# Set-up of a fused attention and soft-MoE kernel: order of the small VectorE steps, and what the first latent products wait for

## The reference, cut to what matters

```python
x = L0_attn_x                                   # (8, 512, 256) float32
x = _layernorm(x + _L0_attn_ref(x, ...), axis=-1)
x = _layernorm(x + _L0_ffn_ref(x, ...), axis=-1)

def _L0_attn_ref(x, ...):                       # 16 heads of 16, latent width 32
    qkv = x @ c_attn_w.T + c_attn_b
    q, k, v = jnp.split(qkv, 3, axis=2)
    q_lat = q @ q2l_w.T + q2l_b                 # k_lat, v_lat likewise with kv2l
    q_lat = q_lat * cos + _rotate_half(q_lat) * sin
    k_lat = k_lat * cos + _rotate_half(k_lat) * sin
    q_for_k = q_lat @ wqk_w.T + wqk_b
    att = softmax(causal(q_for_k @ k_lat^T * L ** (-0.5)))
    y = (att @ v_lat) @ l2o_w.T + l2o_b
    return y @ cproj_w.T + cproj_b

def _L0_ffn_ref(x, ...):                        # 16 experts of 64 slots
    x = _layernorm(x, norm_g, norm_b)
    se = _layernorm(slot_embeds, slot_g, slot_b) * scale
    logits = jnp.einsum('bnd,esd->bnes', x, se)
    ...                                         # dispatch, gated experts, combine
```

## Time and profile before

| | |
|---|---|
| median of 3 runs | 1321.32 us (1320.03 to 1323.57) |
| the profiled execution's own time | 1322.98 us |
| its span, first to last instruction | 1321.3 us |
| PE busy | 1221.5 us, 92% of the span |
| DVE, ACT, POOL busy | 814.6, 681.2, 449.7 us (62%, 52%, 34%) |
| mean granted TensorE clock | 0.957 of full speed |

### The profile page before, as it was taken

One profiled execution on the slowest core, in us unless ns is written; L12 is line 12 of the kernel. 1 busy time (PEld: TensorE's weight loads), 2 busy tenths in 40 slices (PEclk: granted clock), 3 DMA queues, 4 the chain that ended last, 5 costly groups with the idle time before them and its releaser, 6 DMA issues.

```text
span 1321.3 us, 19946 instructions
## 1 busy us (share of the span) xinstructions
PE 1221.5 (92%) x7222; PEld 945.8 (72%) x7222; DVE 814.6 (62%) x1318; ACT 681.2 (52%) x1042; POOL 449.7 (34%) x336
## 2 busy tenths in 40 slices
PE   5799999999999999987799999995999999989996
PEld 4465666666666666654688888884888888879885
DVE  3876697879787978651767777762544444432343
ACT  2445465656565655636477777762555555530111
POOL 5454555465646555402000000000544444430000
PEclk8898999999999999987799999997999999999998
DMA  4644363545445453601043333225655555453771
GB/s 122 138 98 108 89 160 88 150 105 142 117 115 143 113 141 88 160 15 64 33 160 112 112 112 112 96 96 190 201 165 166 162 166 164 136 195 97 226 250 48
DMA packets 121791, 170.32 MB, mean 129 GB/s; under 512 B 47025, under 2 KB 76146, under 8 KB 121714
## 3 DMA queue, kind: packets, MB, share of 16 engines
q1 hardware_dynamic: 120818, 168.74, 44.0%
q10 hardware_dynamic: 896, 0.56, 0.1%
HBM read 72.26 MB, written 37.75 MB: 83 GB/s over the span
## 4 chain that ended last, share of the span: by engine, by line
PE 51%; DVE 3%; ACT 2%; POOL 1%; issue 1%; DMA 1%; ACTq 0%; SPq 0%; POOLq 0%; DVEq 0%
PE ring L376 7%; PE ring L377 7%; PE ring L378 7%; PE ring L1455 6%; PE tail L376 3%; PE tail L378 3%; PE tail L377 3%; PE tail L1455 2%; PE ring L1382 2%; PE ring L1365 2%; PE ring L1372 1%; PE tail L1314 1%; PE tail L1372 1%; PE ring L1336 1%; PE ring L1303 1%
## 5 line engine op out<-in xcount | busy, mean ns | idle before, releaser
L1009 DVE TENSOR_REDUCE mx<-ring 128x4 f32<-128x512 f32 (+2 forms) x192 | 197.9, 1040 | 81.6 <-PE ring L1288 81.1
L749 ACT ACTIVATE pt<-ring 128x1024 f32<-128x1024 f32 (+1 forms) x192 | 169.2, 882 | 151.0 <-PE ring L1303 139.5
L639 POOL TENSOR_SCALAR_AFFINE_SELECT pt<-pt 128x512 f32<-128x512 f32 x128 | 81.2, 635 | 267.0 <-ACT pt L749 266.9
L1303 PE MATMUL ring<-qks 98*128 98x256 f32 (+3 forms) x512 | 132.5, 363 | 15.9 <-DVE mx L1009 7.8
L1286 PE MATMUL ring<-qks 96*128 96x384 f32 (+3 forms) x512 | 142.1, 367 | 1.0 <-DVE x L1035 0.5
L1303 PEld LDWEIGHTS ring<-qks 98*128 98x128 f32 x512 | 78.0, 196 | 75.2 <-DVE mx L1009 32.0
L664 POOL TENSOR_TENSOR hl<-hid,hh 128x512 fp32r<-128x512 f32 x64 | 82.6, 1301 | 77.6 <-ACT hh L850 77.6
L1314 PE MATMUL tail<-pt,va 128*32 128x512 f32 (+3 forms) x1024 | 99.5, 462 | 2.7 <-POOL pt L639 2.7
L1286 PEld LDWEIGHTS ring<-qks 96*128 96x128 f32 x512 | 93.4, 202 | 11.8 <-ACT pt L749 6.5
L1123 DVE SCALAR_TENSOR_TENSOR hid<-ring,bias_e,gate 128x512 f32<-128x512 f32 x64 | 47.9, 748 | 83.9 <-ACT gate L844 49.7
L1288 PE MATMUL ring<-maskb,identb 128*128 128x128 bf16 (+2 forms) x352 | 92.3, 262 | 0.0
(11 more groups left out here) (220 smaller groups left out, 3113.4 us busy)
## 6 DMA issues: line engine op xcount, KB each, us to landing
qks<-stg SPq DMA_DIRECT2D x384, 128.0 KB, 2.4
c_dram<-c2s SPq DMA_DIRECT2D x32, 512.0 KB, 4.8
c<-c_dram SPq DMA_DIRECT2D x32, 512.0 KB, 6.2
sl_dram<-sls SPq DMA_DIRECT2D x32, 256.0 KB, 3.4
sl<-sl_dram SPq DMA_DIRECT2D x16, 512.0 KB, 4.9
wg<-in_wg SPq DMA_DIRECT2D x16, 512.0 KB, 5.6
wu<-in_wu SPq DMA_DIRECT2D x16, 512.0 KB, 6.3
wd<-in_wd SPq DMA_DIRECT2D x16, 512.0 KB, 7.0
```

Of the source, the lines that this page charges most:

```text
L639: nc.gpsimd.affine_select(out=m, in_=m, compare_op=ALU.is_ge, fill=0.0, base=0, pattern=[[0, GH], [1, P]], channel_multiplier=-1).then_inc ...
L749: nc.scalar.activation(pt[j % 2][:, h:h + heads, 0:n], heads_of(tile, heads, n), ACT.Exp, scale=SCALE).then_inc(empty, 1)
L1009: nc.vector.tensor_reduce(out=mx[:, g, i, h:h + heads], in_=heads_of(tile, heads, (i + 1) * P), axis=AX.X, op=ALU.max).then_inc(empty, 1)
L1303: last = nc.tensor.matmul(scores[:, h, :], qks[0:KS_ROWS + 2, g, h0 + h, 1, j * P:(j + 1) * P], qks[0:KS_ROWS + 2, g, h0 + h, 0, j * P:T], ...
```

## The change

It moves DVE's set-up steps, splits two of them, and splits two waits.

1. `bvr` and `kvbr` no longer stand ahead of everything with the wait for `in_small`. They are a step `kvrows`, behind `blat`, which is a step of its own behind `wlat`. The wait for `in_small` moves with it, to `blat`.
2. PE's first `lat` step no longer waits for all 11 set-up instructions. Its w = 0 products wait for a count of 3 (`gbd` and the two w = 0 `wlatl`; `xtl` is waited for by its own semaphore), its w = 1 products for 5.
3. ACT's first read-out `lat` waits for `blat` (a count of 9), which PE's wait covered before.
4. `sestat` is split in two. The first part (scalings, bn_stats, bn_aggr) moves from behind `qlo` of group 0 to ahead of `wv`, behind `cos` of group 0. The second, `sescale` (the 12 tiny instructions), goes from ahead of `cos` of group 1 to behind it.
5. The four transfers of the slot embeddings count in a semaphore of their own, `in_se`, for which `sestat` waits; the other four stay in `in_tail`, for which the first `zT` step now waits too. The order of the transfers on SP is as before.

```diff
-DVE_AT = {"xtl": -29.5, "shuffle": -20.05, "cos": -16.75, "qlo": -10.75, ..., "wlat": -29, "wv": -16.5, "sestat": -10.5, "sel": 8.5}
+DVE_AT = {"xtl": -29.5, "blat": -28.9, "kvrows": -28.8, "shuffle": -20.05, "cos": -16.75, "qlo": -10.75, ..., "wlat": -29, "wv": -16.5, "sestat": -16.6, "sescale": -8.7, "sel": 8.5}
...
-    GBD_DVE, ROWS_DVE, LAT_DVE, WV_DVE, SE_DVE, SETUP_DVE = 1, 3, 11, 12, 12 + 4 + 2 + 3 * NEWTON + 1, 12 + 4 + 2 + 3 * NEWTON + 1
+    GBD_DVE, LOW_DVE, BLAT_DVE, ROWS_DVE, STAT_DVE, WV_DVE = 1, 5, 9, 11, 15, 16
+    SE_DVE = WV_DVE + 2 + 3 * NEWTON + 1
...
                     act.wait_ge(shuffled, group(b, g, 0))
                     act.wait_ge(cosed, group(b, g, 0))
+                    if group(b, g, 0) == 0:
+                        act.wait_ge(setup_dve, BLAT_DVE)
...
-            dve.wait_ge(in_small, IN_SMALL * 16)
-            link(nc.vector.tensor_copy(bvr[:, :, :], bcast(bvc[:, :].unsqueeze(2), [P, NC, P])))
-            link(nc.vector.tensor_copy(kvbr[:, :], bcast(kvb[:, 0:1], [L, P])))
-            assert count[0] == ROWS_DVE
...
+                    assert count[0] == LOW_DVE, count[0]
+                elif name == "blat":
                     dve.wait_ge(lat_made, 3)
+                    dve.wait_ge(in_small, IN_SMALL * 16)
...
+                elif name == "kvrows":
+                    link(nc.vector.tensor_copy(bvr[:, :, :], bcast(bvc[:, :].unsqueeze(2), [P, NC, P])))
+                    link(nc.vector.tensor_copy(kvbr[:, :], bcast(kvb[:, 0:1], [L, P])))
...
                 elif name == "sestat":
-                    dve.wait_ge(in_tail, IN_TAIL * 16)
+                    dve.wait_ge(in_se, IN_SE * 16)
...
+                elif name == "sescale":
                     rsqrt(link, meanvar[:, :, 1], snv[:, :], sny[:, :], snt[:, :])
...
                     if g == 0:
                         pe.wait_ge(x_low, b + 1)
-                        if b == 0:
-                            pe.wait_ge(setup_dve, LAT_DVE)
                     cols = slice(g * P, (g + 1) * P)
                     for w in range(2):
+                        if group(b, g, 0) == 0:
+                            pe.wait_ge(setup_dve, GBD_DVE + 2 * (w + 1))
```

More of the change, by code:

```diff
@@ L37 @@
 ACT_AT = {"xth": -37.25, "lat": -21.0, "khi": -12.1, "qhi": -12.1, "neg": 9.07, "exp": 12.74, "y": 22.75, "yTT": 52.1, "apply": 66.25, "wlat": -30, "senorm": -2, "seT": 7, "seh": 7.1}
-DVE_AT = {"xtl": -29.5, "shuffle": -20.05, "cos": -16.75, "qlo": -10.75, "max": -1.36, "negmax": 5.55, "v": 12.25, "yT": 25.4, "cproj": 53.6, "ln": 57.75, "wlat": -29, "wv": -16.5, "sestat": -10.5, "sel": 8.5}
+DVE_AT = {"xtl": -29.5, "blat": -28.9, "kvrows": -28.8, "shuffle": -20.05, "cos": -16.75, "qlo": -10.75, "max": -1.36, "negmax": 5.55, "v": 12.25, "yT": 25.4, "cproj": 53.6, "ln": 57.75, "wlat": -29, "wv": -16.5, "sestat": -16.6, "sescale": -8.7, "sel": 8.5}
 POOL_AT = {"sin": -23.56, "add": -21.69, "klo": -19.17, "mask": 5.44, "bias": 42}
@@ L65, in order @@
                     add(0, (name, b, c))
-            elif name not in ("wv", "wlat", "senorm", "sestat") or b == 0:
+            elif name not in ("wv", "wlat", "blat", "kvrows", "senorm", "sestat", "sescale") or b == 0:
                 add(SPAN * b, (name, b))
@@ L285, in block_kernel @@
     sem = nc.alloc_semaphore
-    in_lat, in_small, in_rope, in_tail = (sem(n) for n in ("in_lat", "in_small", "in_rope", "in_tail"))
+    in_lat, in_small, in_rope, in_se, in_tail = (sem(n) for n in ("in_lat", "in_small", "in_rope", "in_se", "in_tail"))
     gbd_made, gbd_masked, lat_made, lat_high = sem("gbd_made"), sem("gbd_masked"), sem("lat_made"), sem("lat_high")
@@ L351, in heads_of @@
         return tile[:, :, :].rearrange("p k s -> p (k s)")[:, 0:heads * n].rearrange("p (h n) -> p h n", n=n)
-    GBD_DVE, ROWS_DVE, LAT_DVE, WV_DVE, SE_DVE, SETUP_DVE = 1, 3, 11, 12, 12 + 4 + 2 + 3 * NEWTON + 1, 12 + 4 + 2 + 3 * NEWTON + 1
+    GBD_DVE, LOW_DVE, BLAT_DVE, ROWS_DVE, STAT_DVE, WV_DVE = 1, 5, 9, 11, 15, 16
+    SE_DVE = WV_DVE + 2 + 3 * NEWTON + 1
     POOL_SETUP = 10
-    IN_LAT, IN_SMALL, IN_ROPE, IN_TAIL = 5, 7, 2, 8
+    IN_LAT, IN_SMALL, IN_ROPE, IN_SE, IN_TAIL = 5, 7, 2, 4, 4
     ATTN_CHAIN, COMBINE_CHAIN = G + G + 3 + 1 + 3 * NEWTON, 13
@@ L414, in _ @@
             sp.dma_start(l2b[:, :], a["l2o_bias"]).then_inc(in_small, 16)
[L415 to L418, removed]
+            sp.dma_start(se[:, :, :], a["slots"].rearrange("(n p) d -> p n d", p=P)).then_inc(in_se, 16)
+            sp.dma_start(sg[:, :], a["slot_g"]).then_inc(in_se, 16)
+            sp.dma_start(sb_[:, :], a["slot_b"]).then_inc(in_se, 16)
+            sp.dma_start(ss[:, :], a["scale"].rearrange("(o n) -> o n", o=1).to_broadcast([P, 1])).then_inc(in_se, 16)
             x_t(1)
@@ L960, in _ @@
                                                          scalar1=blr[:, w:w + 1], scalar2=None, op0=ALU.add))
-                    assert count[0] == LAT_DVE, count[0]
+                    assert count[0] == BLAT_DVE, count[0]
+                elif name == "kvrows":
+                    link(nc.vector.tensor_copy(bvr[:, :, :], bcast(bvc[:, :].unsqueeze(2), [P, NC, P])))
+                    link(nc.vector.tensor_copy(kvbr[:, :], bcast(kvb[:, 0:1], [L, P])))
+                    assert count[0] == ROWS_DVE
                     dve.wait_ge(in_rope, IN_ROPE * 16)
@@ L978, in _ @@
                     link(last)
+                    assert count[0] == STAT_DVE, count[0]
+                elif name == "sescale":
                     rsqrt(link, meanvar[:, :, 1], snv[:, :], sny[:, :], snt[:, :])
@@ L1053, in _ @@
                     dve.wait_ge(full, fill_count(st))
+                    if b == 0:
+                        dve.wait_ge(in_tail, IN_TAIL * 16)
                     dve.wait_ge(xn_low, b)
```

## The result

| | before | changed |
|---|---|---|
| median of 20 runs | 1322.25 us | 1318.63 us |
| profiled execution, its own time | 1322.98 us | 1317.78 us |
| its span | 1321.3 us | 1316.1 us |
| first scores (`max` of group 0) start at | 45.71 | 40.74 |

The ratio of the changed kernel to the one before is 0.9969, with a 95% interval of 0.9959 to 0.9979: 4.1 us faster, between 2.8 and 5.4. (One of the 20 runs of the changed kernel was disturbed, at 1534.5 us, and is left out of the ratio.) The prediction had 7.4 us. The time lies in its range and has its sign, but the gain is only about half of the forecast: 0.55 of it by the ratio, and 3.6 us, or 0.49 of it, by the two medians.

A forecast was written before the change was run, and what follows sets the result against it. PE, busy 92% of the span, was taken as the bound: its start 6.9 us earlier, less 2.0 for DVE's queue, until the stack's landing put first scores at 38.3, 7.4 earlier: 1321.32 - 7.4 = 1313.9 us, range 1309 to 1319.

The forecast's parts named there:

- The start: Set-up on DVE and PE: `xtl` runs from 8.0, so PE's first `lat` product starts at 11.85, 5.1 us earlier.
- Rival 1: Set-up on DVE: early `xtl` waits for POOL's memset and ends at 12.5; gain 2.8 us, time 1318.5; chance 0.18.
- The statistics' price: DVE ahead of `wv`: `sg` waits for POOL's `sin` until 21.0, the rest takes 3.7; costs 2.0 of 6.9 us.
- The lower bound of the forecast: Statistics on DVE: if bn_stats wait for POOL's `add` until 23.4, DVE is 2.3 later; gain 5.1 us (1316.2).
- The clock: PE's set-up: group 0's twelve products at full clock need 2.9 us instead of 4.7 and end 6.9 earlier.
- The price at half: PE's set-up: with the half clock at the start the gain is 5.6 us instead of 7.4 (1315.7).
- The stack decides: Before the first scores: group 0's 12 transfers land 9.7 us after their start, at 38.3; scores 7.4 us earlier.
- bn_stats take no wait: Statistics on DVE ahead of `wv`: bn_stats beside a POOL product are not held, so no time is added.
- rival 2: Before the first scores: the stack lands sooner, only `wqk` of group 1 holds PE; 10.8 us earlier, 1310.5; chance 0.05.
- Rival 3: Behind the first scores: a later wait eats the earlier start, time stays at 1321.3; chance 0.05.
- Rival 4: PE's later stages: more falls to half clock, each costing 5 us; with three more 1329; chance 0.06.

The follow-up runs named there:

- e2: Changed kernel with the start put back to the old order, leaving only the moved statistics; ratio 1.0014 to the kernel before, 1.9 us slower.
- e7: Changed kernel with the scaling of `sb_` alone moved to the head of `sescale`; ratio 0.9945 to the kernel before, gain 7.3 us.
- e8: Changed kernel with `sb_` following `sg` without waiting for it; ratio 0.9960 to the kernel before, gain 5.3 us.
- e10: Changed kernel run again without an edit; ratio 0.9969 to the kernel before, gain 4.1 us.
- e1: Changed kernel without its move of the statistics, so the new start alone; ratio 0.9960 to the kernel before, gain 5.3 us.
- e3: Changed kernel with the scalings of `sg` and `sb_` moved to the head of `sescale`; ratio 0.9946 to the kernel before, gain 7.1 us.
- e4: Changed kernel with all of `sestat` and `sescale` behind `cos` of group 1; ratio 0.9945 to the kernel before, gain 7.3 us.
- e6: As e3, but the two scalings are done by ACT ahead of `senorm`, none on DVE; ratio 0.9957 to the kernel before, gain 5.7 us.
- e9: As e3, with four of the twelve transfers of group 0's stack issued by ACT; ratio 0.9950 to the kernel before, gain 6.6 us.
- e11: e3 repeated without a further edit; ratio 0.9941 to the kernel before, gain 7.8 us.
- e5: Changed kernel with PE's first `lat` products waiting for all four `wlatl`; ratio 0.9988 to the kernel before, gain 1.6 us.

## Why the prediction was right and where it failed

- **The start**: right but for 0.46 us. `xtl` at 7.99 with 1.23 us (8.0 forecast), PE's first product at 12.31 (11.85, since the set-up products ahead took 1.48 us instead of 1.03), the second wait without cost, `bvr` and `kvbr` hidden.
- **Rival 1, the memset**: fell. `xtl` ran wholly inside it. The Trainium skill's rule (SBUF — State Buffer, Who interferes with whom), that two SBUF inputs contend only with a GpSimd instruction that reads SBUF, agrees with this trace: 1.23 us wholly under the memset, against 1.34 before, behind it. And the row of `bvr`, on which the rival rested, was that of a copy: 0.86 us at the memset's end, 0.29 now; in e2 it began at 10.67, took 0.63 and ended at 11.30 as before. The measured median, 1318.63, is all but this rival's 1318.5; that is chance, as its mechanism did not happen.
- **The statistics' price**: here the prediction failed. It had `sg` waiting 2.25 for `sin` (measured 2.31, right) and then put "from `sb_` to the end of the averages" at 3.7 us, taken from a stretch in which POOL was idle. `sb_` is of the same kind as `sg`, and POOL's `add` stood directly behind `sin`. The term was 2.15 us too small. With it the sum is 7.4 - 2.15 = 5.2 us, and the first scores of the first profile show 5.0; most of the rest is the 0.46 us of the start. The lower bound of the forecast, 5.1 us, comes close by luck: it was made for bn_stats waiting until `add` ended, and no bn_stats waited. e7 and e8 take away this wait alone and get 38.09 and 37.93 for a forecast of 38.3.
- **The clock**: "I take the full clock" held in one profile of the changed kernel and not in the other. The price at half, 1.8 us, stood in the text as a bound; measured were 2.1 us (42.87 against 40.74). What the prediction left out: it read half rate at 16.95 as the effect of the idle stretch, which fits that profile (the set-up products ahead had reached full rate, 1.03 us), and concluded that PE straight out of other work has the full clock. In e10 it had not, as the first rise had not come. Between 5.0 (rise in time) and 45.71 - 42.87 = 2.8 (rise late) lies the measured 4.1. Of the ten profiles with the changed start (the changed kernel twice, e1, e3, e4, e6 to e9, e11) only e10 has the late rise. If one execution in ten loses 2.1 us, the mean loses 0.2, an estimate from few profiles; so the late rise alone does not make 5.0 into 4.1, a difference that lies within the interval.
- **The stack decides**: right. It landed 9.67 us after its first issue (9.7), `wqk` of group 1 was done before, and the new wait of 2.15 us in front of the scores is its landing (that it is as long as the missed wait of `sb_` is chance).
- **bn_stats take no wait**: right, shown by e3 and e7.
- **Rivals 2, 3 and 4**: rival 2 needed a faster landing, which even two queues did not bring. Rival 3 is excluded by the interval. Rival 4 had no support: the mean granted clock of the two profiles is the same, 0.957, and from 45 to 150 us, where the earlier trace rows lie, it was 0.93 against 0.90 before.

In most rows of the table the measured gain lies under that of the scores: by 0.3 to 3.0 us, and in e8 (7.8 us of scores, at most 7.0 by its interval) and e9 (9.6, at most 9.1) beyond the interval. e3's profile was 10.6 us ahead at the first `zT` and 8.7 at its end. Where the rest is lost is open; one profile a kernel can't tell a later stage from chance.

## What to carry to other kernels

Before a small instruction is moved on DVE, look up what POOL does at its new place, for each such instruction in turn: here a two-element scaling cost as much as the POOL product that it met. A series whose members depend on each other can lose the turn to POOL more than once. In these traces bn_stats and bn_aggr (e3), `shuffle` (1.34 us beside POOL's `klo` in e3) and `wvh`, which reads PSUM (0.69 beside `add` in e3, 0.69 without a POOL product in the changed kernel), stood beside POOL for nothing; the others belong where nobody waits behind them. And ask what decides once the old wait is gone: here a transfer with 2.5 us of slack took over, and `wqk` of group 1, 8.1 us earlier (44.65 to 36.54), brought scores only 5.0 us earlier.

## What the runs showed of the hardware that was not expected

- DVE and POOL take turns by whole instructions, whatever the size: 128x2 elements took 2.3 to 2.4 us where they met a whole POOL product (`sg` and `sb_` in the changed kernel and in e2, `sb_` in e3), and the wait on DVE's own last instruction, 0.03 us of the timeline, was enough to lose the turn (e8). POOL waits likewise: `sin` of group 0, begun under DVE's `cos` (18.13 to 19.33), took 3.16 us, `sin` of group 1 2.34. Tiny instructions with two inputs wait too: 2.20 us for 128x8 elements in e6, 0.17 alone.
- The recorded granted clock is not to be trusted at the start of the program: 1.00 in the record, products 0.43 to 0.45 us apart as at 1.2 GHz (e5, e10, and e2 from 17.51 to 21.78), where 0.23 is the spacing at 2.4 GHz. In the kernel before the record had 0.50 for the same spacing from 17 to 20 us. The start times of equal products show the clock better than the record. The Trainium skill (TensorE: Matmul & The Clock Gate, Part 1: The HAM clock gate) has half rate as the default state, and warns that clock events in a trace may be unreliable; these three profiles agree with both.
- The first rise, read from the spacing, came near 16.6 us in e10, where PE had not stood still since its first product, near 18.9 in e5 behind 0.80 us of standing, and by 12.5 in the nine other profiles with the changed start. The set-up of the changed kernel thus differed by 2.1 us between two executions.
